# Four attention layers and a scan layer in a twelve-layer fp32 network on one core: late chunks projected among the scores, a double norm in one pass, key products left in PSUM

## The reference

```
# f1, f2: 32 heads of 4, every token sees every token, then an expert mlp; a second norm inside
x = x + 0.5 * _L1_ffn_ref(_layernorm(x), ...)
    xn = (x - mu) / jnp.sqrt(var + 1e-05) * ln_g + ln_b          # x is the outer norm's result
    q, k, v = xn @ wq, xn @ wk, xn @ wv
    p = softmax(einsum('bqhd,bkhd->bhqk', q, k) / sqrt(hd))
    o = einsum('bhqk,bkhd->bqhd', p, v).reshape(B, S, D) @ wo + x
    h = gelu(einsum('metd,edf->metf', xe, w1) + b1)              # xe: o, split among experts
    y = einsum('metf,efd->metd', h, w2) + b2
# a1, a2: 16 heads of 8, causal, rotated q and k
x = x + _L2_attn_ref(_layernorm(x), Wq, Wk, Wv, Wo)
    xq_out = xq * cos + rotate_half(xq) * sin                    # and xk likewise
# l3: decayed linear attention in both directions; a second norm inside
x = x + _L3_attn_ref(_layernorm(x), ...)
    x_n = _ln(x, ln1_w, ln1_b)
    phi_q, phi_k = elu(q) + 1, elu(k) + 1;  lam = max(sigmoid(x_n @ dec_w + dec_b), 1e-8)
    forward:  S = S * l_t + k_t * v_t;        out_f = q_t . S
    backward: R = l_t * (k_t * v_t + R);      out_b = q_shift . R
    out = out_f + out_b;  num, den = out[:K], max(out[K:], 1e-6);  attn = num / den
```

## Time and profile before

| | us |
|---|---|
| median of 3 runs | 3429.65 (3427.45 to 3430.12) |
| the profiled execution | 3427.32 |
| its span in the trace | 3425.6 |
| mean granted TensorE clock | 0.912 |

### The profile page before, as it was taken

How to read it: one execution, slowest core, us unless ns; L and a number is a source line. 1 busy time by engine, 2 the same in 40 slices (tenths; PEclk the granted TensorE clock), 3 DMA queues, 4 the chain that set the end, 5 groups by cost and what they waited for, 6 DMA issues and landing times. The chain is left out here.

```text
span 3425.6 us, 43749 instructions
## 1 busy us (share of the span) xinstructions
PE 2895.8 (85%) x15972; PEld 1094.5 (32%) x15972; DVE 2371.4 (69%) x3143; ACT 1825.5 (53%) x3733; POOL 494.6 (14%) x830
## 2 busy tenths in 40 slices
PE   5999897899999997489858999999885799685668
PEld 2443343122222225233322222222262233261235
DVE  5554546899999973566658999999535666547951
ACT  2215322388888883156534888888742366442012
POOL 0000002100110000222221100100012222221210
PEclk9999998699999998699977999999997799897778
DMA  3210121200000000111112000000001111100000
GB/s 116 90 38 1 44 90 54 89 18 18 18 19 23 19 22 23 63 38 46 33 49 75 18 23 20 18 18 18 29 5 54 41 47 34 29 1 23 0 0 13
DMA packets 59354, 118.14 MB, mean 34 GB/s; under 512 B 14267, under 2 KB 33980, under 8 KB 55685
## 3 DMA queue, kind: packets, MB, share of 16 engines
...
## 5 line engine op out<-in xcount | busy, mean ns | idle before, releaser
L1173 DVE TENSOR_REDUCE arena<-ps 128x1 f32<-128x1024 f32 (+7 forms) x1536 | 1572.6, 1064 | 293.5 <-PE ps L834 204.8
L1044 ACT ACTIVATE arena<-ps 128x512 f32<-128x512 f32 (+3 forms) x2816 | 1382.8, 573 | 393.1 <-PE ps L882 392.0
L828 PE MATMUL ps<-arena 61*128 61x512 bf16 (+4 forms) x2816 | 957.0, 385 | 125.1 <-DVE arena L1173 48.8
L882 PE MATMUL ps<-arena 64*128 64x512 bf16 (+4 forms) x2816 | 746.8, 372 | 73.8 <-ACT arena L1044 33.3
L854 PE MATMUL ps<-arena 128*32 128x512 f32 (+3 forms) x5632 | 712.8, 578 | 1.4 <-POOL arena L1132 1.2
L882 PEld LDWEIGHTS ps<-arena 64*128 64x128 bf16 (+1 forms) x2816 | 205.9, 95 | 806.3 <-ACT arena L1044 558.5
L828 PEld LDWEIGHTS ps<-arena 61*128 61x128 bf16 (+1 forms) x2816 | 259.6, 96 | 471.5 <-DVE arena L1173 366.2
L332 PE MATMUL ps<-xnT,moe_up 128*128 128x512 f32 x480 | 230.3, 605 | 0.0
L518 DVE TENSOR_TENSOR arena<-arena,ps 128x512 f32<-128x512 f32 x120 | 82.2, 686 | 156.7 <-ACT arena L448 129.8
L448 ACT ACTIVATE arena<-ps 128x512 f32<-128x512 f32 x120 | 71.4, 597 | 222.9 <-PE ps L332 222.8
L1100 POOL TENSOR_TENSOR arena<-arena,ones 16x128 bf16<-16x128 f32 x96 | 42.8, 446 | 860.0 <-ACT arena L1029 755.0
...
## 6 DMA issues: line engine op xcount, KB each, us to landing
...
f_o<-arena SPq DMA_DIRECT2D x256, 10.0 KB
```

The lines of the kernel that those rows point to most:

```text
L828: last = nc.tensor.matmul(at[:, k0 // CHUNK, 0:n], score_rows(Qop[par], j, slice(q0, q0 + P)), score_rows(Kop[par], j, slice(k0, k0 + n)), ...
L882: nc.tensor.matmul(ps[:, ring_bank(item), off:CHUNK], shifted_rows(Kop[par], j, slice(kb * P, (kb + 1) * P)), shifted_rows(Qop[par], j, sl ...
L1044: nc.scalar.activation(pr[:, (at % 2) * 4 + j, off:CHUNK], ps[:, ring_bank(item), off:CHUNK], ACT.Exp).then_inc(s.ex, 1)
L1173: nc.vector.tensor_reduce(mq[:, half, j * 4 + qb:j * 4 + qb + 1], src, AXX, ALU.max).then_inc(s.sread, 1)
```

## The change

**Late chunks among the scores.** In f1, a1, f2, a2 chunks 0 and 1 are projected and cut ahead of the scores. Chunks 2 and 3 follow among the first 16 score pairs: PE places project(2, side) behind pair 3 and 5, the values of 2 and the turning of chunk 3 behind 6, project(3, side) behind 8 and 10, the values of 3 behind 12; DVE puts the rotations and remainders ahead of maxima 5, 7, 10 and 12. Buffers for rotation, remainder and cut parts are doubled (chunk modulo 2), and chunk 1 is projected into the score banks. SP's order is: store 0, store 1, load(0, 0), load(1, 1), store 2, store 3, put_max.

**The double norm as one.** Where a layer norms twice, the statistics are taken once from x and rstd is (var(1 + eps) + eps^2)^-1/2, which applied to x gives the second norm's result. The outer result, needed as residual, is made apart: in f by outer_apply on DVE behind the last unit, in l3 by ACT during the scans. The calls of the next layer's first norm in other layers use the same formula.

**The tail.** Out-projections of chunks 0 and 1 move into steps 4 to 11 of the last unit, one group of 128 columns a step, and DVE's order becomes outer_apply (f only), quotients 0 and 1, copies 0 and 1, quotients 2 and 3, copies 2 and 3.

**The scans.** The key product stays in PSUM, written over the values, and both scans read it there. bw has three buffers. There is no sum: POOL multiplies fw and bw apart, and PE gathers both into the same banks. The values of an item wait until the backward scan of the item two ahead has read its banks.

```diff
+        def outer_apply(dve, s, ch):
+
+            dve.wait_ge(s.rstd1, ch + 1)
+            for n in range(TPC):
+                last = nc.vector.tensor_scalar(res_rows(ch)(n), x_rows(ch)(n), mv[:, ch, n, 0:1],
+                                               rstd1[:, ch, n:n + 1], ALU.subtract, ALU.mult)
+            return last
...
+            if double:
+                t.settle(pool, nc.gpsimd.tensor_scalar(var[:, b, :], mv[:, b, :, 1], 1.0 + EPS, EPS * EPS,
+                                                       ALU.mult, ALU.add))
...
-                for ch in range(CHUNKS):
+                def store_cut(ch):
                     b, t0 = ch // 2, (ch % 2) * CHUNK
                     for side, to in ((0, qs), (1, ks)):
                         sp.wait_ge(s.cut2, 2 * ch + side + 1)
                         for part in range(3):
                             sp.dma_start(to[b * HG:(b + 1) * HG, part, :, t0:t0 + CHUNK],
-                                         cut[side][:, part, :]).then_inc(cut_stored[b][side], 16)
-                    if ch == 1:
-
-                        sp.wait_ge(s.qst0, 16 * 3 * CHUNKS // BATCH)
-                        sp.wait_ge(s.kst0, 16 * 3 * CHUNKS // BATCH)
-                        sp.wait_ge(s.kneg, 1)
-                        load(0, 0)
-                    if ch == 2:
-                        put_max(0, 0, 0)
+                                         cut[ch % 2][side][:, part, :]).then_inc(cut_stored[b][side], 16)
+
+                store_cut(0)
+                store_cut(1)
+                sp.wait_ge(s.qst0, 16 * 3 * CHUNKS // BATCH)
+                sp.wait_ge(s.kst0, 16 * 3 * CHUNKS // BATCH)
+                sp.wait_ge(s.kneg, 1)
+                load(0, 0)
                 sp.wait_ge(s.kneg, 2)
                 load(1, 1)
+                store_cut(2)
+                store_cut(3)
+                put_max(0, 0, 0)
...
+            def proj_bank(ch, side):
+                if rope:
+                    return {1: 0, 2: 2}.get(2 * ch + side, PROJ)
+                return (2 if ch == 1 else PROJ) + side
...
+                        if u == UNITS - 1 and 4 <= at < 4 + 2 * TPC:
+                            out_project((at - 4) // TPC, (at - 4) % TPC)
...
                 pe.wait_ge(s.ops0, 16 * N_OPS)
                 for k in range(16):
                     scores(-1, 0, 0, k)
+                    if k in (3, 5):
+                        project(2, k // 4)
+                    if k == 6:
+                        project_values(2)
+                        norm_tensor(pe, s, 3, TURNED)
+                    if k in (8, 10):
+                        project(3, k // 10)
+                    if k == 12:
+                        project_values(3)
                 turn_max(0, S_SLOT)
...
+                    between = {5: [lambda: rotate(2, 0)], 7: [lambda: rotate(2, 1), lambda: remainders(2)],
+                               10: [lambda: rotate(3, 0)], 12: [lambda: rotate(3, 1), lambda: remainders(3)]}
+                maxima(0, 0, between)
...
+                if double:
+                    for ch in range(CHUNKS):
+                        last = outer_apply(dve, s, ch)
+                    t.settle(dve, last)
+                quotient(0)
+                quotient(1)
+                projected(0)
+                projected(1)
+                if not double:
+                    dve.wait_ge(s.x, 1)
+                    ahead_stats(dve, s, t, CHUNKS, after)
+                quotient(2)
+                if not double:
+                    ahead_apply(dve, s, CHUNKS, after)
+                quotient(3)
+                projected(2)
+                projected(3)
...
+                    w = sel[:, e, :] if e < 8 else same
+                    pe.wait_ge(s.fq, n + 1)
                     if b and e == 8:
                         pe.wait_ge(s.dn, 1)
                     if b and e == 0:
                         pe.wait_ge(s.oT, 1)
                     for h in range(2):
-                        w = sel[:, e, :] if e < 8 else same
+                        nc.tensor.matmul(ps[:, (4 if e < 8 else 6) + h, :], w,
+                                         fw[:, n % 3, h * CHUNK:(h + 1) * CHUNK],
+                                         start=e in (0, 8), stop=False, skip_group_check=True)
+                    pe.wait_ge(s.bq, n + 1)
+                    for h in range(2):
                         last = nc.tensor.matmul(ps[:, (4 if e < 8 else 6) + h, :], w,
-                                                fw[:, n % 3, h * CHUNK:(h + 1) * CHUNK],
-                                                start=e in (0, 8), stop=e in (7, 8),
-                                                skip_group_check=True)
+                                                bw[:, n % 3, h * CHUNK:(h + 1) * CHUNK],
+                                                start=False, stop=e in (7, 8), skip_group_check=True)
                     last.then_inc(s.acc, 1)
...
                 for n in range(18):
-                    pool.wait_ge(s.g, n + 1)
-                    nc.gpsimd.tensor_tensor(fw[:, n % 3, :], fw[:, n % 3, :],
-                                            phq[:, n // 9 * SEQ:(n // 9 + 1) * SEQ], ALU.mult)\
-                        .then_inc(s.gq, 1)
+                    bb = slice(n // 9 * SEQ, (n // 9 + 1) * SEQ)
+                    pool.wait_ge(s.fw, n + 1)
+                    nc.gpsimd.tensor_tensor(fw[:, n % 3, :], fw[:, n % 3, :], phq[:, bb], ALU.mult)\
+                        .then_inc(s.fq, 1)
+                    pool.wait_ge(s.bw, n + 1)
+                    nc.gpsimd.tensor_tensor(bw[:, n % 3, :], bw[:, n % 3, :], phq[:, bb], ALU.mult)\
+                        .then_inc(s.bq, 1)
...
-                        nc.vector.scalar_tensor_tensor(
-                            kv[:, k, :],
-                            ps[:, 2 * (v % 2):2 * (v % 2) + 2, :].rearrange("p b t -> p (b t)"),
-                            col("l3_vb", item - 1), phk[:, bb], ALU.add, ALU.mult).then_inc(s.vr, 1)
-                        dve.wait_ge(s.vr, v + 1)
+                        nc.vector.scalar_tensor_tensor(src, src, col("l3_vb", item - 1), phk[:, bb],
+                                                       ALU.add, ALU.mult).then_inc(s.kv, 1)
+                        dve.wait_ge(s.kv, v + 1)
                     else:
-                        t.settle(dve, nc.vector.tensor_copy(kv[:, k, :], phk[:, bb]))
+                        src = phk[:, bb]
                     if n >= 3:
                         dve.wait_ge(s.acc, n - 2)
-                    nc.vector.tensor_tensor_scan(fw[:, n % 3, :], lam[:, bb], kv[:, k, :], 0.0,
-                                                 ALU.mult, ALU.add)
-                    t.settle(dve, nc.vector.tensor_tensor_scan(
-                        bw[:, k, 0:SEQ - 1][:, ::-1], kv[:, k, 1:SEQ][:, ::-1],
-                        lam[:, b * SEQ + 1:(b + 1) * SEQ][:, ::-1], 0.0, ALU.add, ALU.mult))
-                    nc.vector.tensor_tensor(fw[:, n % 3, :], fw[:, n % 3, :], bw[:, k, :],
-                                            ALU.add).then_inc(s.g, 1)
+                    nc.vector.tensor_tensor_scan(fw[:, n % 3, :], lam[:, bb], src, 0.0,
+                                                 ALU.mult, ALU.add).then_inc(s.fw, 1)
+                    nc.vector.tensor_tensor_scan(
+                        bw[:, n % 3, 0:SEQ - 1][:, ::-1], src[:, 1:SEQ][:, ::-1],
+                        lam[:, b * SEQ + 1:(b + 1) * SEQ][:, ::-1], 0.0, ALU.add, ALU.mult)\
+                        .then_inc(s.bw, 1)
```

357 lines of the change are left out of this document (180 added, 177 removed).

## The result

| | before | after |
|---|---|---|
| median, 4 runs each | 3429.6 (3427.5 to 3430.1) | 3379.1 (3377.0 to 3382.2) |
| ratio | | 0.9855 (95%: 0.9838 to 0.9872) |
| span of the profiled execution | 3425.6 | 3375.3 |

A forecast was written before the change was run, and what follows sets the result against it. No engine fills the span; the limit changes by stage, DVE bounding l3's scans. 3427.3 - 33 - 2.5 - 8.4 (f heads) - 11 (a heads) + 5 - 2 (tails) = 3375.4; the median lies 2.3 above, given as 3377.5, range 3350 to 3400.

The forecast's parts named there:

- The scans: l3's scans: sum and most stalls removed, cadence 5.85 for 8.01; -36.0, with +3 for clock restarts -33 (-24 to -38).
- the +3 for PE's clock restarts: l3's scans: PE idles in each 6.55 us reciprocal; three or four clock restarts at about 1 us cost +3.
- Rival 1: l3's scans: scans still wait for POOL's multiply, 9.2 an item, scans 18 longer; 3428, no change; chance 0.05.
- l3's projections: l3: second norm goes, shortening PE's waits for DVE's xn in three of four chunks; -2.5 (0 to -6).
- Heads of f: f1, f2: first score 6.5 earlier (5.2 to 7.2), late chunks then give back +2.3; net -4.2 each.
- Heads of a: a1, a2, heads with rotation: unit 0 starts 7.0 earlier, memsets cost +1.5; net -5.5 each (-1 to -10).
- first score 5.8 earlier: a1, a2: chunk 1 gets free banks and no wait for chunk 0's rotation; first score 5.8 earlier (4 to 7).
- that load has landed: a1, a2: second unit's load, now ahead of chunks 2 and 3's stores, has landed; PE's 10.74 wait goes.
- The +1.5 for the memsets: a1, a2: three 1024-column memsets, formerly hidden under PE's wait for the second unit's operands, delay DVE's first maxima by 1.5.
- Tails of f: f1, f2: eight out-projection pieces of 0.45 (+3.6), quotient wait +1.7, 2.8 won at the end; +2.5 each (-3 to +5).
- The 2.8 won at the end: f's tails: one chunk instead of two behind the last quotient and no queue of copies; 2.8 of 18.8 won.
- rival 5: All heads at their best bound and tails at no cost: 3350; up to it within the forecast's 0.80, beyond it 0.04.

The follow-up runs named there:

- scan_sbuf: Changed kernel with only the key product written to SBUF, so both scans read two SBUF operands, still without the sum: 3422.2 us, one run.
- tail_late: Changed kernel with out-projections of chunks 0 and 1 behind the last unit again, DVE's new order of quotients and copies kept: 3361.0 us, ratio 0.9804.
- sp_old: Changed kernel with the heads' order on all engines and SP's order both as before the change: 3373.0 us, one run.

## Why the forecast held, and where its steps did not

**The scans (-33, measured -39.0).** The mechanism held as written: no sum, no stall, the sixteen forward scans at one length, POOL keeping up (89.6 us in multiplies, forecast about 85). The 6 us between forecast and measurement have three parts. PSUM costs a scan nothing (2286 against 2291 ns), where I gave it 0.05, and the cadence is 5.69 for 5.85: 2.6 over sixteen. 1.3 were won between DVE's last work on an item and the last quotient, which the sum left out, and item 9, whose backward scan took 4.36, took about 1 of this back. And the +3 for PE's clock restarts was wrong. They occur, but the slower matmuls are hidden: behind the first reciprocal a value pair took 3.72, the next one 1.88 again, and DVE waited for none.

```profile
3149.83 3.72 PE L1834 MATMUL ps<-xnT,arena 128*128 128x512 f32 x4 [8.11 <-DVE arena L2010]
...
3156.82 1.88 PE L1834 MATMUL ps<-xnT,arena 128*128 128x512 f32 x4
```

Values are made two items ahead (these are needed at 3155.38), and that slack takes it up. The Trainium skill (VectorE: DVE Perf Modes, the section on the TRN2 errata) has 120 fixed cycles for a PSUM source against 58, by my estimate 0.065 us more; the scans here don't show it. The product does not settle it: with a PSUM source it takes 1268 ns, 44 more than the sum of the same width from SBUF (1224), but is another operation. Rival 1 fell for the reason given with it, and scan_sbuf shows what it described when the operand is in SBUF. The Trainium skill (SBUF — State Buffer, "Who interferes with whom") has a DVE instruction with two SBUF inputs contend with a GpSimd one that reads SBUF, and scan_sbuf agrees: both multiplies and the backward scan last 4.3, the forward scan 3.1.

**l3's projections (-2.5, measured -4.3)** lie within their bounds. The stretch behind the quotient (nothing, measured -1.4) was not in the sum. There PE's clock falls to the low level 5 us behind the quotient's start (at 3248.9), before it was 3 (at 3295.8); that may be part of it.

**Heads of f (-6.5 and +2.3, measured -7.8 and +2.1, -7.2 and +1.8).** Right in place, and in size but for f1's -7.8, outside the bound of 7.2. PE's first transposes now start with the block instead of 5.2 behind it:

```profile
568.74 0.66 PE L268 MATMUL ps<-ident,xn 128*128 128x128 f32 x4 [2.51 <-DVEq L203]
```

No run puts the second norm back, so its share is read from the stages alone. That chunk 2 was free before, under the load, was in the prediction; that chunk 3 could be free there too, with PE now idle for 21.5 us ahead of f1's first score, was not.

**Heads of a (-5.5 each, measured -3.1 and -1.6 from the block's start to the first reciprocal).** The step that failed is "first score 5.8 earlier": it came 2.4 and 3.7 earlier. Chunk 1 is cut 7 us earlier (its last remainder ends 22.4 after the block's start, 29.4 before), but the first load is issued only 2.4 earlier. I took the stores as unchanged. Their DMA view in a1, from first store to load's issue (40 slices), before and after:

```profile
GB/s 0 0 25 66 80 86 91 79 79 95 95 79 98 95 97 81 97 97 36 0 0 0 0 29 77 82 95 91 68 84 86 88 93 93 95 97 86 97 97 18
```

```profile
GB/s 0 0 21 39 82 78 86 95 76 80 97 89 74 89 97 95 95 80 89 99 95 72 82 97 95 86 84 89 97 97 74 89 95 93 82 86 91 93 95 12
```

Before, the two chunks' stores (1.57 MB together) were two bursts with a gap; now they run into one another at some 90 GB/s and last 20 us. The transfer became the limit. The half with late chunks came to 32.1 in a1, with a granted clock of 0.77, and to 33.8 in a2 (forecast 31.5). The +1.5 for the memsets did not show: from unit 0 to the first reciprocal a1 took 0.4 less than before and a2 0.5 more.

**Tails of f (+2.5, measured +3.3 and +7.1).** The term that was too small is the piece: 0.64, not 0.45, 1.5 over eight. The wait of 1.5 was in the sum as 1.7, but not the lower clock that can follow it: 1.5 us in this f2 (38.3 for 36.8), and 5 in f1 in three of five executions of the same code. The 2.8 won at the end is there in f1 (3.4), and tail_late shows it is DVE's. In f2 it left 0.6: the experts' first 16 matmuls took 5.44 for 3.72 us, at first at half clock. PE had waited 8.92 for the quotient ahead of them, but 8.82 in f1, which did not lose it, so the cause stays open. Tails of a: forecast -1, measured -0.7 and +0.5.

**What cancelled.** The four layers gave 10.5 less than forecast, of which a's first scores are 5.5 and f's tails 5.4; l3 gave 9 more, 6 of it in the scans. None of these was foreseen as making up for another. Of the prediction's bounds, 3350 for rival 5 does not follow from its terms: heads at their best and tails at no cost give some 3360; 3350 takes the scans (-38) and the projections (-6) at their best as well.

**SP's order** was priced right in kind ("that load has landed"), but not by its size: 13 us in each a layer by sp_old, which the late chunks among the scores then spent again (sp_old 3373.0, changed kernel 3379.1).
